# Graph convolutions: one PSUM block per step, added by VectorE step by step

## What is computed

```
deg  = segment_sum(ones, dst);  dinv = where(deg > 0, rsqrt(max(deg, 1)), 0)
def gcn_conv(x, W, b):
    h   = x @ W
    msg = h[src] * (dinv[src] * dinv[dst])[:, None]
    return segment_sum(msg, dst) + b
x = layernorm(x + gcn_conv(relu(gcn_conv(x, W1, b1)), W2, b2))
```

## Time and profile before

| | |
|---|---|
| median of three runs | 15060.8 us (15028.1 to 15099.16) |
| the profiled execution | 15005.17 us, its span 15003.3 us |
| first convolution's loops | about 10274 to 12590 us of the span |
| second convolution's loops | about 12640 to 14930 us |
| everything before the convolutions | the first 10270 us |

### The profile page before, as it was taken

The page is one execution under the profiler, slowest core; times in us unless marked ns, Lnnn a source line. Parts: engine busy times, 40 slices in busy tenths (PEclk is TensorE's granted clock), DMA queues, the critical chain, the costliest instruction groups (busy, mean ns, idle before and its releaser), DMA issues.

```text
span 15003.3 us, 181666 instructions
## 1 busy us (share of the span) xinstructions
PE 8287.5 (55%) x46670; PEld 7635.5 (51%) x46671; DVE 6679.2 (45%) x13205; ACT 2744.9 (18%) x6542; POOL 9034.8 (60%) x8046
## 2 busy tenths in 40 slices
PE   5777777754555555578856555563333334333334
PEld 5777777754444444467745455463333333333333
DVE  6444444434444444479956556574222223222223
ACT  0111111101111111156633334341000000000000
POOL 3888888874555555510017777774666664666664
PEclk7666666667677777789967767675555555555555
DMA  5333333332333333333212222231111111111111
GB/s 91 18 18 18 18 18 18 18 50 80 91 91 92 91 91 91 91 100 99 98 49 69 64 66 71 63 79 31 23 23 23 23 23 26 23 23 23 23 23 23
DMA packets 851085, 769.36 MB, mean 51 GB/s; under 512 B 652784, under 2 KB 660804, under 8 KB 848965
## 3 DMA queue, kind: packets, MB, share of 16 engines
q0 software_dynamic: 446272, 333.87, 16.8%
q1 hardware_dynamic: 371597, 322.68, 6.8%
q10 hardware_dynamic: 33170, 112.27, 2.3%
HBM read 569.49 MB, written 197.82 MB: 51 GB/s over the span
## 4 chain that ended last, share of the span: by engine, by line
issue 23%; another core or an unknown queue 18%; PE 13%; DVE 12%; SPq 10%; POOL 10%; DMA 9%; DVEq 4%; ACT 0%; ACTq 0%; POOLq 0%
POOL lane_tab L667 8%; DMA lane_tab<-rows,idx 8%; SPq L562 7%; PE ps L1129 3%; PE ps L1144 3%; DVE buf_c L1519 2%; SPq L424 2%; DVE acc_w L1773 1%; DVEq L447 1%; DVEq L458 1%; PE ps L1232 1%; PE ps L1213 1%; PE ps L1168 1%; PE ps L1154 1%
## 5 line engine op out<-in xcount | busy, mean ns | idle before, releaser
L691 POOL DMA_INDIRECT tab<-gcn_tab,idx x3136 | 2986.0, 952 | 1718.5 <-issue 1148.2
L667 POOL DMA_INDIRECT lane_tab<-rows,idx x1664 | 2599.8, 1562 | 616.2 <-issue 613.5
L691 POOL DMA_INDIRECT tab<-att_tab,idx x1568 | 1762.5, 1124 | 1928.3 <-DVEq L1660 1330.1
L1144 PE MATMUL ps<-tab,buf_d 128*128 x3328 | 794.4, 387 | 2171.3 <-issue 2118.7
L1144 PEld LDWEIGHTS ps<-tab,buf_d 128*128 128x128 f32 x3328 | 782.0, 320 | 2283.8 <-issue 2283.7
L1773 DVE TENSOR_TENSOR acc_w<-acc_w,ps 128x512 f32 x416 | 286.3, 688 | 3422.0 <-remote 2957.1
L681 POOL DMA_INDIRECT buf_b<-src_tab,idx x832 | 834.2, 1003 | 802.5 <-DVEq L1522 339.5
L681 POOL DMA_INDIRECT acc_w<-src_tab,idx x832 | 840.0, 1010 | 654.9 <-DVEq L1522 399.9
L1103 PE MATMUL ps<-tab,buf_d 128*128 x3328 | 892.6, 361 | 354.5 <-DVEq L1523 331.7
L1043 PE MATMUL ps<-ident,srcg 128*128 128x128 f32 x3328 | 723.1, 405 | 656.2 <-DVE srcg L1406 653.5
L1144 PEld LDWEIGHTS ps<-tab,buf_a 128*128 128x128 f32 x3328 | 726.0, 330 | 652.9 <-issue 652.6
(11 more groups left out here) (283 smaller groups left out, 17226.4 us busy)
## 6 DMA issues: line engine op xcount, KB each, us to landing
y_stash<-buf_c SPq DMA_DIRECT2D x208, 512.0 KB
tab<-y_stash SPq DMA_DIRECT2D x208, 512.0 KB, 3.3
aux<-in_edge_attr_dram SPq DMA_DIRECT2D x1696, 32.0 KB
aux<-dst_rows ACTq DMA_DIRECT2D x104, 512.0 KB
buf_b<-dst_rows ACTq DMA_DIRECT2D x104, 512.0 KB
tab<-gcn_tab,idx POOLq DMA_INDIRECT x3136
lane_tab<-rows,idx POOLq DMA_INDIRECT x1664
tab<-att_tab,idx POOLq DMA_INDIRECT x1568
```

Source lines behind the costliest of these rows:

```text
L667: pool.indirect_dma_start(lane_tab[k][:, :], bass.IndirectOffsetOnAxis(ap=idx[:, b, u:u + 1], axis=0), rows[:, b, u, 0:D1], None, compute_ ...
L691: pool.indirect_dma_start(to[k][:, u, :], None, table[:, :], bass.IndirectOffsetOnAxis(ap=idx[:, k % RING, u:u + 1], axis=0)).then_inc(row ...
L1144: last = pe.matmul(ps_flat[:, bass.ds(rel[u] + q * 512, D)], g_hot[q][:, u, :], g_ring[:, bass.ds(at[u], D)], start=False, stop=True, skip ...
```

## The change

TensorE no longer zeroes the bank and no longer places its products by window. Product u of a group goes to columns 64u to 64u + 63 of the bank, at a fixed address, and starts its own sum there. So TensorE reads nine registers and not 17 per group. VectorE reads eight registers (the windows of the eight steps) and not one, and adds the eight blocks of 64 columns one after the other to their windows. As two steps may belong to one window, each add waits for the one before it. The bank's semaphore is counted by these adds: it goes up by eight per group, and TensorE waits for all eight. A wait for the cleared accumulator is added ahead of each convolution's loop.

```diff
+        def load_places(g):
+            _, v = nc.values_load_multi_w_load_instructions(
+                g_places[:, bass.ds(g * GP + G, G + 1)], engines=(mybir.EngineType.PE,), min_val=0, max_val=(LONG * G - 1) * D,
+                skip_runtime_bounds_check_because=PLACES_WHY)
+            return v[0:G], nc.s_assert_within(v[G], RING + 1, RING * (TT + 1))
...
                 with pe.Fori(0, TURNS) as i:
                     for q in range(RING):
                         g = i * RING + q
-                        pe.wait_ge(free, g + 1)
-                        pe.matmul(ps[:, q, :].rearrange("p (k f) -> p k f", f=P), zero_b[:, :],
-                                  bc(ident_b[:, :].unsqueeze(1), [P, 4, P]), start=True, stop=False, skip_group_check=True)
+                        pe.wait_ge(free, g * G + G)
+                        pe.sem_inc(s.passed, 1)
                         pe.wait_ge(left_ready, g + 1)
-                        rel, at, needed = load_steps(g)
+                        at, needed = load_places(g)
                         pe.wait_ge(landed, needed)
                         for u in range(G):
-                            last = pe.matmul(ps_flat[:, bass.ds(rel[u] + q * 512, D)], g_hot[q][:, u, :], g_ring[:, bass.ds(at[u], D)],
-                                             start=False, stop=True, skip_group_check=True)
+                            last = pe.matmul(ps[:, q, u * D:(u + 1) * D], g_hot[q][:, u, :], g_ring[:, bass.ds(at[u], D)], start=True, stop=True)
                         last.then_inc(done, 1)
...
             def gcn(conv, hot, outs, bank_free, order):
                 twice(twice_g, w12[:, conv, :])
                 dve.memset(acc_w[:, :, :], 0.0).then_inc(order, 1)
-                dve.sem_inc(bank_free, RING)
+                dve.wait_ge(order, 1)
+                dve.sem_inc(bank_free, RING * G)
                 dve.sem_inc(outs, AHEAD)
...
-                        w0 = load1(mybir.EngineType.DVE, win_s, g, W - 1)
+                        ws = load8(mybir.EngineType.DVE, win_s, g, W - 1)
                         dve.wait_ge(outs, g + (AHEAD + 1))
-                        a = acc_w[:, bass.ds(w0, G), 0:D]
-                        dve.wait_ge(order, g + 1)
-                        dve.tensor_tensor(a, a, ps[:, q, :].rearrange("p (k f) -> p k f", f=D), ALU.add).then_inc(order, 1)
-                        dve.wait_ge(order, g + 2)
-                        dve.sem_inc(bank_free, 1)
+                        for u in range(G):
+                            a = acc_w[:, bass.ds(ws[u], 1), 0:D].rearrange("p a f -> p (a f)")
+                            dve.tensor_tensor(a, a, ps[:, q, u * D:(u + 1) * D], ALU.add).then_inc(bank_free, 1)
+                            dve.wait_ge(bank_free, g * G + (RING * G + u + 1))
```

## The result

The kernel after takes 15187.35 us (median of 20 runs, 15107.18 to 15436.26), the kernel before 15063.74 us (20 runs beside them, 15005.35 to 15128.38). The longest run of the kernel after is one in a slower state of the chip; the ratio leaves it out, and without it the median is 15176.31 us. The ratio is 1.0072, with a 95% interval of 1.0055 to 1.0089: some 108 us slower. The forecast was 15055 us and no change. The kernel did get slower, by an amount that is clear of the noise, so "no change" was wrong; the time lies on the side of the first rival.

The account below looks back on a forecast made before the run. It took POOL's gathers, 40.1 of each 45.8 us plus a pause per 32, as the bound. Last groups -14 us and ends +5 us made -9, 15052 us against the runs' median; forecast 15055, range 14,860 to 15,400.

Parts of the forecast that it names:

- no change: Whole kernel: time within 0.5%, 75 us, of the kernel before; chance 0.52.
- the first rival: VectorE starved by 0.70 us sequencer steps beside gathers, beyond about 41 instructions per group; +110 to +320 us, likeliest 15,270; chance 0.26.
- a turn without disturbance: VectorE's work per group, back to back: from 2.6 to 5.2 us, range 4.0 to 6.7.
- The ends: Behind each convolution's last gathers: 5.2 instead of 5.8 us per group, -14 us; later last adds and added wait, +5 us.
- the wait behind the cleared accumulator: Ahead of each convolution's loop: the extra wait behind the clearing costs under 0.3 us.
- the chain within a turn: After a POOL pause: VectorE's matrices and TensorE's products done in 14.1 us, 12 to 17, so the pause recurs unchanged.
- the 17 quick microseconds: First rival's count: VectorE's steps stay quick for some 17 us after each mid-convolution restart, then take 0.70 us each.
- the 29 us of slack: Between TensorE's products being done, 14.1 us after the restart, and the next signal being seen, 45.8 us after the first.
- A: Theory tested by the experiments: VectorE has a budget of sequencer instructions per gather restart, overdrawn by 45 per group.
- The signal is no longer late: Rival: TensorE's shorter register load frees its late count and POOL's pauses go; -566 us, 14,490, or nearer -60; chance 0.20.
- TensorE's finish slips past a point: Rival: TensorE's count comes after POOL has restarted, so POOL stops again; +340 us, 15,400; chance 0.07.

Follow-up runs that it names:

- e1: Kernel before with only TensorE's half: no zeroing product, fixed columns, nine registers, VectorE still adding the bank once; 15056.17 us against 15068.99, ratio 0.9987.
- e8: Kernel after without POOL's gathers in the two convolutions, run once; a convolution's adds take 1025 us, 4.9 us per group.
- f1: Kernel after, unchanged, on a chip of the fast kind; 13338.66 us, ratio 1.0001 to the kernel before there.
- f3: Kernel before with each group's eight target columns copied once to a fixed place, on a fast chip; 13369.06 us, ratio 1.0004.
- e4: Kernel after with the eight comparisons of a group as one instruction on 128 x 1024; ratio 1.0026 to the kernel before.
- e6: Kernel before with VectorE adding the bank in two halves of 256 columns, a wait after each; ratio 1.0013.
- e2: Kernel before with only VectorE's half: eight adds of 64 columns to neighbouring windows, a wait after each; 15190.76 us, ratio 1.0066.
- e3: Kernel before with 24 empty semaphore increments more per group on VectorE; ratio 1.0087.
- e7: Kernel before with eight adds of 64 columns on VectorE to different windows and one wait behind them; ratio 1.0016.
- e5: Kernel before with the eight comparisons of a group as one instruction on 128 x 1024; ratio 1.0005.

## Why the prediction was wrong

**What held.** During the gathers the zeroing product and the shorter register load are worth nothing (e1's gathers took 4 us less in 4479): TensorE had time, as the forecast said. Behind the last gathers they speed TensorE up to 3.3 to 3.9 us per group, as forecast. Its nine registers take 2.17 us at the median and 0.70 at the quick end (1.97 and 0.78 forecast), VectorE's eight 0.60 (0.59). An add of 64 columns is 222 ns (225 forecast). The formula in the Trainium skill's VectorE: DVE Perf Modes, TRN2 errata, gives (64 + 151)/0.96 = 224 ns as an estimate, and this trace agrees, at a size where the forecast had no row. Eight adds are 2.77 us (3.0 forecast) and a turn without disturbance 4.9 in the mean of e8 (5.2).

**Two small terms that were wrong.** The ends cost 12.9 + 6.6 us in the profiled pair, where 5 was forecast for both and 14 were to be won. First, the pace before was read from two adds, 5.80 us apart. The other groups behind the last gathers are faster: the first three adds follow at 2.6 to 3.3 us, every fourth after that at 3.8, and the last twelve come 5.3 us apart in the mean. With VectorE at 4.9 us for all of the 16 groups left, the last add comes 80.7 us after the last gather and not 73.1: a loss of some 7 us at each end and no gain. Second, the wait behind the cleared accumulator was put at "under 0.3". It holds the first gathers back by 4.5 and 5.5 us. On the fast kind of chip, f1 against f3, the same two give some 7 + 2 us (42.6 against 35.8 between the convolutions, 88.1 against 86.3 behind the last gather).

**The step that failed** is the chain within a turn: "After, DVE needs 2 x 5.2 = 10.4 us, from 8 to 13.4, and PE 3.7 us more: 14.1 us [...]. So 29 us of slack stay, and the pause should recur unchanged." It took VectorE's turn at its quick pace throughout. In the stretch shown the slow steps began 8 us after VectorE went on, TensorE's products were finished after 21.8 us, and POOL had stopped after 16 gathers. The pause did not recur unchanged: 190 pauses and 642 us in place of 107 and 570, and 84 us more from first to last gather.

The first rival had this mechanism, and was held back to 0.26 by two of its own numbers. One is the count: "Its loop grows from about 25 to 38 instructions per group (two per compare, two per add, six others), or 46 if each add's wait is a step of its own." It is, and the trace has 44.6. The forecast leaned on 38 because it let the wait ride on the address step ("I take 0.15, as the wait can ride on the address step"). For the duration that was near enough, 0.14 us between two adds. The other is the 17 quick microseconds after a restart: the earlier trace rows show one stretch, and in 30 of the 95 restarts of the same trace that meet slow steps these begin 7.0 to 7.8 us after it. In the kernel after they begin 6 to 11 us after most restarts.

The rival's threshold, "more than about 41 instructions per group", lies where the loss sets in, but the loss sets in gradually: the gathers took 3 us longer at 26.6 instructions, 32 at 37.6, 72 to 84 at 44.6 and 111 at 48.0, and the turn grew along with them. The trace of the kernel before had the evidence for the count, in the source of the line where VectorE waits for a group's products:

```profile
L1770 DVEq ALU_OP  x416: 4/40/1384, 10281.1 to 14921.8; - x139
```

One step of arithmetic per group, for a wait whose value depends on the loop's index. (Other waits of the loop share such a value and have 104 steps or none; eight waits for eight values can't share.)

**What was too simple in it.** The rival took the quick stretch after each restart as a time. Within one kernel it is nearer to a number of instructions. In the kernel before 62 to 93 of VectorE's were issued between POOL's restart and the first slow step, 7 to 29 us later. In the kernel after it was 53 to 80, 6 to 11 us later, behind 155 of the 191 restarts; behind 20, mostly after short pauses, it was 22 or fewer, and 16 stretches had none. But it is no fixed number either: in e4 it was more than 100 behind 55 restarts, up to 172 and 41 us, and in e1, where VectorE's code is that of the kernel before, 62 to 68 behind 89 of 96 restarts and not 30 of 95. So A's "budget" describes the kernels with small instructions, and what sets it is open. Nor do slow steps cost anything by themselves: e1 and e6 have some 980 of them on VectorE, nearly twice those of the kernel before (some 540), and neither lost time. TensorE's sequencer has them too, 1121 in e1. And the 29 us of slack belonged to a stretch of 32 gathers: with a pause after 16 or 24, TensorE's products are due at once. Against that, the price was kept down by something that the forecast did not see either: a pause for a late product is shorter (3.2 us, 112.0 / 35) than one for a late signal (5.6 us), and POOL's stopping gives VectorE its quick steps back, mostly 1 to 4 us after the stop. Nearly twice the pauses at 3.4 us cost 642 us against 570. Hence +108 us by the ratio, at the low end of the 110 to 320 that the rival had, and not the 15,270 that it held most likely; some 24 of the 108 us are the ends and the wait behind the clearing, which the rival didn't have.

**The other rivals.** The signal is no longer late: false, e1 leaves it as it was. TensorE's finish slips past a point: in part, since 35 pauses wait for TensorE's products; but it slips because VectorE's matrices come late, and e1, with TensorE's half alone, has none of them.

**What is not settled.** Why VectorE's steps become slow beside gathers, why TensorE's signal is seen late, and why both are absent on three chips and present on another with the same program. Shown is that VectorE's half makes the loss (e2, e1), that instructions which do no work are enough for it (e3), and that the slow steps need gathers (e8) and aren't always there with them (f1). That the number of instructions counts, and not only the time they take, rests on e4 beside e7 and on the slow stretches themselves, where most steps take 0.70 us whether they take 57, 40 or 21 ns otherwise. That the slow steps end when POOL stops is what the traces look like, not what an experiment varied by itself. A kernel with a turn of 4.9 us but few instructions, and with gathers of 0.95 us, would tell count from length; none was run.

## What to carry to other kernels

Before an instruction on a loaded engine is split, count what its sequencer gets and not only what the engine executes: an address that depends on a register and a wait for a value that depends on the loop are instructions too, and here they made three out of one. Take their cost from start to start and not from their duration: an empty step of 21 ns had its next 93 ns later. An engine that is idle for most of the time can still have no room for them while indirect gathers run. And when a kernel's whole time differs by a tenth between two chips, find out which of its waits exist on only one of them before a few tenths of a per cent are argued about.

## What the runs showed of the hardware

- **VectorE's sequencer has two speeds beside indirect gathers.** 57 and 40 ns a step, and 0.70 us a step, with nothing in between that lasts. The slow one mostly came after 53 to 93 instructions since the gathers' restart (before and after; up to 172 in e4) and mostly ended 1 to 4 us after they stopped. Without gathers (e8), and on the faster chips with them (f1), all of some 9950 steps in each took 57 or 40 ns. TensorE's sequencer shows the slow steps as well (1121 in e1's convolutions). The Trainium skill's Runtime: NRT & Kernel Launch, Instruction fetch mechanics, says that the fetch of instructions is hidden because the sequencer issues more slowly than its memory is refilled. Whether the slow steps are fetches no run here shows. The profile of the kernel after counts 47 transfers of the kind "instruction" in the whole execution, beside some 2000 slow steps of VectorE, so there isn't one such transfer per slow step.
- **The same program takes 15,070 us on one chip and 13,326 to 13,362 on three others.** The gathers of a convolution take 2239 us on the one and 1962 to 1969 on the others, at the same 0.95 us each and the same granted clock of 0.50. The difference there is pauses; the time up to the first convolution differs too, 10,275 to 10,411 against 9,272 to 9,326 us. Whether it is the chip, or what else its machine did at the time, is open.
- **A large comparison on VectorE makes the gathers beside it longer.** With 128 x 1024 tensor_tensor comparisons a gather takes 1.00 us in the mean and not 0.95 (e4, e5), with 128 x 128 tensor_scalar ones of the same elements it doesn't: 153 to 160 us over 3136 gathers, enough to cancel what shorter pauses gave back.
